# Graph attention on one core: probabilities turned by DMA transposes instead of TensorE, and heads stacked by VectorE

## What is computed

```python
h = jnp.maximum(_layernorm(x, axis=-1), 0.0)
q, k, v = (_heads(h @ W + b) for W, b in ((Wq, bq), (Wk, bk), (Wv, bv)))
scores = jnp.einsum('bhqd,bhkd->bhqk', q, k) / np.sqrt(HEAD_SIZE)
bias = jnp.where(graph_mask, 0.0, NEG)[:, None]
probs = jax.nn.softmax(scores + bias, axis=-1)
ctx = jnp.einsum('bhqk,bhkd->bhqd', probs, v)
out = x + (ctx.transpose(0, 2, 1, 3).reshape(b, s, H) @ Wf + bf)
```

## Time and profile before

| | |
|---|---|
| median of 3 runs | 702.35 us (701.69 to 703.3) |
| profiled execution, first to last instruction | 701.6 us |
| mean granted clock of TensorE | 0.985 |
| bytes moved by DMA | 61.36 MB, 87 GB/s over the span |

### The profile page before, as it was taken

How to read it: one execution, slowest core, us unless ns; L and a number is a source line. 1 busy time by engine, 2 the same in 40 slices (tenths; PEclk the granted TensorE clock), 3 DMA queues, 4 the chain that set the end, 5 groups by cost and what they waited for, 6 DMA issues and landing times.

```text
span 701.6 us, 21244 instructions
## 1 busy us (share of the span) xinstructions
PE 677.3 (97%) x7156; PEld 562.7 (80%) x7156; DVE 555.2 (79%) x1676; ACT 464.9 (66%) x972; POOL 270.1 (39%) x330
## 2 busy tenths in 40 slices
PE   7688999999999999999999999999999999999996
PEld 5466888888888888888888888888888888888874
DVE  5748887887887878788787878878787887888785
ACT  2545676767677676767767676776767677676763
POOL 1334444334444433444443344444334444333420
PEclk8899999999999999999999999999999999999998
DMA  5123333433332343333234333323433332343220
GB/s 187 43 52 89 101 72 89 105 85 90 90 98 71 90 105 84 90 92 96 71 91 105 84 87 94 90 74 94 105 81 89 95 88 75 95 105 78 65 71 35
DMA packets 72453, 61.36 MB, mean 87 GB/s; under 512 B 17649, under 2 KB 72434, under 8 KB 72434
## 3 DMA queue, kind: packets, MB, share of 16 engines
q1 hardware_dynamic: 72434, 61.12, 33.8%
HBM read 17.05 MB, written 12.58 MB: 42 GB/s over the span
## 4 chain that ended last, share of the span: by engine, by line
PE 90%; issue 3%; DVE 3%; DMA 1%; ACT 1%; POOL 1%; SPq 0%; POOLq 0%; DVEq 0%
PE ring L767 17%; PE ring L769 17%; PE ring L768 17%; PE probs_t L834 11%; PE scores L824 6%; PE scores L825 6%; PE ctx L850 3%; PE ctx L852 3%; PE ctx L851 3%; PE ring L779 3%; PE ring L860 3%; DMA w_raw<-in_L_gnn_Wv_dram 1%; ACT probs L404 0%; DMA x_in<-in_x_dram 0%; DVE w_lo L623 0%
## 5 line engine op out<-in xcount | busy, mean ns | idle before, releaser
L404 ACT ACTIVATE probs<-logits,least 128x256 f32<-128x256 f32 x384 | 175.1, 504 | 78.0 <-DVE least L536 77.0
L354 POOL TENSOR_TENSOR split<-qk,split 128x512 f16<-128x512 f32 x96 | 111.3, 1160 | 274.9 <-DVE split L559 274.9
L409 ACT ACTIVATE pt_hi<-probs_t 128x512 f16<-128x512 f32 x192 | 114.6, 597 | 108.1 <-PE probs_t L834 107.3
L536 DVE CUSTOM_DVE_ANT_0 logits<-scores,mask,logit_unscale 128x256 f32<-128x256 f32 x384 | 169.1, 478 | 4.5 <-PE scores L825 3.7
L767 PE MATMUL ring<-h_hi,w_hi 128*128 128x256 f16 x576 | 158.3, 275 | 2.0 <-DVE w_lo L623 1.5
L768 PE MATMUL ring<-h_lo,w_hi 128*128 128x256 f16 x576 | 158.1, 275 | 0.0
L769 PE MATMUL ring<-h_hi,w_lo 128*128 128x256 f16 x576 | 158.0, 274 | 0.0
L543 DVE SCALAR_TENSOR_TENSOR pt_lo<-probs_t,pt_hi 128x512 f16<-128x512 f32 x192 | 131.6, 686 | 0.7 <-ACT pt_hi L409 0.6
L834 PE MATMUL probs_t<-ident,probs 128*128 128x128 f32 x768 | 116.4, 274 | 5.4 <-ACT probs L404 5.3
L559 DVE CAST split<-qk 128x512 f16<-128x512 f32 x96 | 41.3, 430 | 98.3 <-ACT qk L422 98.3
L422 ACT ACTIVATE qk<-ring,qk_bias_s,qkv_ratio 128x256 f32<-128x256 f32 x192 | 96.7, 552 | 15.2 <-PE ring L769 15.2
(11 more groups left out here) (86 smaller groups left out, 1300.0 us busy)
## 6 DMA issues: line engine op xcount, KB each, us to landing
heads<-split SPq DMA_DIRECT2D x192, 96.0 KB, 2.2
x_in<-in_x_dram SPq DMA_DIRECT2D x32, 384.0 KB, 3.3
heads<-split SPq DMA_DIRECT2D x192, 64.0 KB, 2.1
out_dram<-result SPq DMA_DIRECT2D x64, 192.0 KB, 1.9
adj_in<-in_adj_dram SPq DMA_DIRECT2D x32, 64.0 KB, 2.0
w_raw<-in_L_gnn_Wq_dram SPq DMA_DIRECT2D x1, 576.0 KB, 4.1
w_raw<-in_L_gnn_Wk_dram SPq DMA_DIRECT2D x1, 576.0 KB, 6.5
w_raw<-in_L_gnn_Wv_dram SPq DMA_DIRECT2D x1, 576.0 KB, 6.3
```

The lines of the kernel that those rows point to most:

```text
L404: act.activation(probs[u % 2][:, a], logits[u % 2][:, a], ACT.Exp, bias=least[u % 2][:, a:a + 1], scale=-1.0).then_inc(probs_ready, 1)
L536: dve.tensor_tensor_reduce(out=logits[u % 2][:, a], in0=score_bank[u % 2][:, a * S:(a + 1) * S], in1=mask[b.parity][:, t], scale=logit_uns ...
```

## The change

Six parts, all in one:

1. The turn of the probabilities leaves PE. `exps` now computes p x 2^14 directly (its bias is `least` plus ln 2^14, made per unit by a small ACT instruction into `raised`). ACT `probs_hi` splits off the high part and POOL `probs_lo` the low part, both from SBUF and with queries still in the partitions, into `p_rows[u]` (128 x 1024 f16, 256 KB). SP then issues one DMA transpose per unit, which writes `p_cols[u]`. DVE's `probs_lo` is gone.
2. `apply_probs` comes four slots after the scores (`LAG = 4`) instead of two, and everything behind it moves accordingly: `divide`, `transpose_context`, `project_out` and `finish` of a batch are done in the next cycles, and there is one cycle more at the end (`B + 2`).
3. The heads of all three pairs are stacked by DVE, `copy_heads`, four copies of 64 partitions per pair (two of 768 columns and two of 512), in place of the twelve DMAs.
4. `x_in` and `residual` have four buffers (`RING`) instead of two, `h_hi` and `h_lo` two, `logits`, `least` and `probs` three, and the loop turns four batches at a time.
5. The two PSUM banks of the turned probabilities go to the ring of the projections (five banks).
6. The order within the cycles is rewritten on all five engines; `project_v(b, 1)` moves into batch b's own first slot, and `layer_stats` looks three batches ahead, in two parts.

The diff, cut to its core:

```diff
@@
+            def transpose_probs(b, u):
+
+                wait(sp, p_lo_ready, b.count(UNITS, u + 1))
+                alone(sp)
+                sp.dma_start_transpose(p_cols[u][:].rearrange("p w a s q -> p (w a s) q"),
+                                       p_rows[u][:].rearrange("p w a k -> p (w a k)")).then_inc(p_placed[u], 16)
@@
+            def probs_lo(b, u):
+                wait(pool, p_hi_ready, b.count(UNITS, u + 1))
+                pool.tensor_tensor(p_rows[u][:, 1], probs[u % 3][:], p_rows[u][:, 0],
+                                   ALU.subtract).then_inc(p_lo_ready, 1)
@@
             def exps(b, u):
 
+                wait(act, p_lo_ready, b.count(UNITS, u - 2))
+                wait(act, logits_ready, b.count(2 * UNITS, 2 * u + 2))
+                alone(act)
+                act.activation(raised[u % 3][:], least[u % 3][:], ACT.Identity,
+                               bias=p_raise[:, 0:1]).then_inc(raised_ready, 1)
+                wait(act, raised_ready, b.count(UNITS, u + 1))
@@
             def probs_hi(b, u):
-                wait(act, pt_ready, b.count(UNITS, u + 1))
-                act.activation(pt_hi[u % 2][:].rearrange("p a t q -> p (a t q)"), pt_bank[u % 2][:],
-                               ACT.Copy, scale=P_SCALE).then_inc(pt_hi_ready, 1)
+                wait(act, probs_ready, b.count(2 * UNITS, 2 * u + 2))
+                act.activation(p_rows[u][:, 0], probs[u % 3][:], ACT.Copy).then_inc(p_hi_ready, 1)
@@
                 if u == 0:
                     wait(dve, mask_ready, b.count(2, 2))
+                wait(dve, probs_ready, b.count(2 * UNITS, 2 * u - 4))
@@
-            def probs_lo(b, u):
-                wait(dve, pt_hi_ready, b.count(UNITS, u + 1))
-                dve.scalar_tensor_tensor(
...
+            def copy_heads(b, j):
+
+                wait(dve, qk_lo_ready, b.count(C, j + 1))
+                for a in range(2):
+                    own = slice(D * a, D * a + D)
+                    other = slice(D - D * a, 2 * D - D * a)
+                    dst, src = heads[b.parity][:, 2 * j + a], split[j]
+                    dve.tensor_copy(dst[own], src[own, 1:4]).then_inc(heads_copied, 1)
+                    dve.tensor_copy(dst[other, 0:2], src[own, 0:3:2]).then_inc(heads_copied, 1)
@@
             def scores(b, u):
                 t, j = u // C, u % C
                 if t == 0:
-                    wait(pe, heads_placed[j], b.count(4 * 16, 4 * 16))
+                    wait(pe, heads_copied, b.count(4 * C, 4 * (j + 1)))
                 wait(pe, logits_ready, b.count(2 * UNITS, 2 * u - 2))
@@
-            def transpose_probs(b, u):
-                wait(pe, pt_lo_ready, b.count(UNITS, u - 1))
...
             def apply_probs(b, u):
                 t, j = u // C, u % C
-                wait(pe, pt_lo_ready, b.count(UNITS, u + 1))
+                wait(pe, p_placed[u], b.count(16, 16))
@@
+                def attend(u):
+
+                    if here:
+                        scores(b, u)
+                    if u < LAG:
                         if before:
-                            transpose_probs(b + -1, UNITS - 1)
+                            apply_probs(b + -1, UNITS - LAG + u)
                     elif here:
-                        transpose_probs(b, u - 1)
+                        apply_probs(b, u - LAG)
```

More of the change, by code:

```diff
@@ L23 @@
+import math
 from contextlib import ExitStack
@@ L376, in cycle @@
             def cycle(b):
-                first, front = b.k == -1, (b + 1).exists()
+                here, before, front = b.exists(), (b + -1).exists(), (b + 1).exists()
+                first = b.k == -1
+                if here:
+                    split_lo(b, 2)
+                if before:
+                    probs_lo(b + -1, 5)
+                if here:
+                    probs_lo(b, 0)
+                if (b + 2).exists():
+                    normalise(b + 2)
+                if here:
+                    probs_lo(b, 1)
                 if front:
@@ L380, in cycle @@
                     split_lo(b + 1, 0)
+                if here:
+                    probs_lo(b, 2)
+                if front:
                     split_lo(b + 1, 1)
-                    if not first:
-                        add_bias(b + 1)
-                if (b + 2).exists():
-                    normalise(b + 2)
-                if front:
-                    split_lo(b + 1, 2)
                     if first:
@@ L391, in cycle @@
                         pool.wait_ge(bf_ready, 1)
-                        add_bias(b + 1)
+                if here:
+                    probs_lo(b, 3)
+                if front:
+                    add_bias(b + 1)
+                if here:
+                    probs_lo(b, 4)
             cycles(pool, cycle)
@@ L588, in finish, with layer_stats @@
                 dve.scalar_tensor_tensor(out=result[t][:], in0=R_OUT[t][:, 0:H], scalar=out_unscale[:, 0:1],
-                                         in1=residual[b.parity][:, t], op0=ALU.mult,
+                                         in1=residual[b.slot][:, t], op0=ALU.mult,
                                          op1=ALU.add).then_inc(result_ready, 1)
-            def layer_stats(b):
-                wait(dve, x_loaded[b.parity], b.dma_count())
-                for t in range(QT):
-                    dve.bn_stats(out=stats[:, t], in_=x_in[b.parity][:, t]).then_inc(moments, 1)
+            def layer_stats(b, parts):
+                if 0 in parts:
+                    wait(dve, x_loaded[b.slot], b.dma_count(RING))
+                for t in parts:
+                    dve.bn_stats(out=stats[:, t], in_=x_in[b.slot][:, t]).then_inc(moments, 1)
+                if 1 not in parts:
+                    return
                 for t in range(QT):
@@ L784, in project_qk @@
                     wait(pe, h_lo_ready, b.count(2, 2))
-                if j == 2 and 0 in parts:
-                    wait(pe, qk32_ready, b.count(2 * C, 4))
+                if 0 in parts and j > 0 and (b + -1).exists():
+                    wait(pe, v_lo_ready, (b + -1).count(2, j))
                 for n in parts:
@@ L865, in project_out @@
                 wait(pe, ct_lo_ready, b.count(2, t + 1))
-                if t == 1 and (b + 2).exists():
-                    wait(pe, qk32_ready, (b + 2).count(2 * C, 2))
                 for c in range(C):
@@ L909, in cycle @@
-                if here:
-                    scores(b, 0)
-                transpose_of(0)
-                apply_of(0)
+                        apply_probs(b, u - LAG)
+                attend(0)
                 if front and not first:
                     transpose_h(b + 1)
+                if here:
+                    project_v(b, 1)
+                attend(1)
+                if front:
+                    project_qk(b + 1, 0)
+                attend(2)
+                if before:
+                    transpose_context(b + -1, 0)
```

362 lines of the change are left out of this document (158 added, 204 removed).

## The result

The changed kernel is **slower by 13%**. Its four runs took 810.72, 810.55, 798.5 and 794.03 us, against a median of 702.83 us for the kernel before on the same chip. The ratio is 1.1323 (interval 1.1281 to 1.1365), taken from the two shorter runs, so about 796 against 703, while the profiled execution is one of the two longer ones (810.55 us, span 808.8, clock 0.92 against 0.94). The forecast was 743 with a range of 640 to 850.

A forecast was written before the change was run, and what follows sets the result against it. PE set the 20.60 us period before; DVE was to bound the changed kernel at 16.3 work + 5.4 waits = 21.7 us. 32 x 21.7 + 42.4 start and drain + 5 ends + 0.75 to the median = 743 us, range 640 to 850.

The forecast's parts named there:

- PE, removed: Turns of probs leave PE: 2.64 us a batch saved, PE's need falls from 20.60 to 17.96 us, 617 us at best.
- The forecast's base: Period before the change, from 20 batches in 412.0 us: 20.60 us a batch, set by PE alone.
- ACT and POOL: Added splits and `raised`: ACT rises from 14.36 to 17.4 us a batch, POOL from 8.36 to 15.3, both under 17.96.
- The copies: Twelve head copies a batch on DVE: 3.9 us, less 0.07 overlap each, so 3.1; DVE's work 16.3 us.
- the low end: DVE copies move four f16 columns at a time: 0.36 and 0.29 us, against 0.96 and 0.69 at the high end.
- DVE against POOL: DVE's copies and casts wait for POOL's wide operations at the shared port: 5.4 us a batch, range 0 to 19.7.
- The step that failed: DVE's work plus waits, 16.3 + 5.4 = 21.7 us a batch, taken as the period, making DVE the bound.
- SP and the DMA engines: Six transposes a batch replace twelve heads DMAs: 1.0 to 8.4 us each, taken as hidden by the lag of some 7 us.
- Rival 1: Copies find the port free; faster if waits stay below 4.1 us a batch, 647 us at 2.4; chance 0.33.
- Rival 2: DMA transposes bound the kernel if each takes over 3.6 us; 855 us at 4.2 us each; chance 0.10.
- rival 3: Gain and loss cancel at waits of about 4.1 us a batch, nothing measurable (about 0.2%); chance 0.03.
- What would show it: Signs: PE some 83% busy, idle before `scores` from DVE, copies 0.7 us or more, casts over 0.43, POOL about 490 us.

The follow-up runs named there:

- e16: Changed kernel with heads of pairs 0 and 1 by DMA ahead of the transposes, pair 2 by VectorE, loop written out; 685.01 us, ratio 0.9756 to the kernel before.
- e4: Kernel before, with only the heads stacked by VectorE copies instead of DMAs, the copies ahead of the rest in their slots; 806.14 us, ratio 1.1459.
- e1: Changed kernel with GpSimd's low part of the probabilities left out but for two columns; 734.12 us, ratio 1.0413 to the kernel before.
- e5: Changed kernel with `ct_lo` put first in slot 4 on VectorE, ahead of result and copies; 765.27 us, ratio 1.0893 to the kernel before.
- e6: Changed kernel with the low part of the probabilities on VectorE instead of GpSimd; 834.16 us, ratio 1.1875 to the kernel before.
- e9: Changed kernel with `ct_lo` first in slot 4 and the copies of pair 0 ahead of the cast; 782.39 us, ratio 1.1121 to the kernel before.
- e13: Changed kernel with `ct_lo` first in slot 4 and GpSimd's residual behind the low part there; 762.32 us, ratio 1.0841 to the kernel before.
- e15: Kernel before, with only the heads stacked by VectorE copies, the copies behind the rest in their slots; 888.37 us, ratio 1.2636.
- e14: Changed kernel with eight matmuls nobody reads on TensorE ahead of the second output projection; 772.29, 772.49 and 778.1 us, ratio 1.1016 to the kernel before.
- e8: Changed kernel with all heads by DMA again and GpSimd's low part cut to two columns; 725.08 us, ratio 1.0323 to the kernel before.
- e2: Changed kernel with the heads stacked by twelve DMAs a batch again, GpSimd's low part kept; 726.86 us, ratio 1.0337 to the kernel before.
- e10: Changed kernel with heads of pairs 0 and 1 by DMA ahead of the transposes, pair 2 by VectorE; 701.45 us, ratio 0.998 to the kernel before.
- e18: Kernel before with the loop written out; 703.04 us, ratio 0.9992 to the kernel before.

## Why the prediction was right in its direction and wrong in its size

**PE, removed.** Right as a term, never seen as time: 768 matmuls are gone, and in e16 TensorE is busy for 374.71 of 400 us, 18.3 of its period of 19.5 us, against the forecast 17.96. The forecast's base is 0.1 us off: the 412 us of the earlier trace rows hold 20.1 batches, since `rstd` starts at 200.99 and at 405.99 us, ten batches apart, so the period before was 20.50 us and not 20.60. The 3 us that this takes from 32 periods go to start and drain, so the sum stands.

**ACT and POOL.** Right: `raised` takes 296 ns (forecast 0.29), ACT's split 626 (forecast 710), GpSimd's low part 1170 (forecast 1160); GpSimd's busy time is 507 us (forecast about 490).

**The copies.** Right in the time of one: 0.34 to 0.36 and 0.29 us (forecast 0.36 and 0.29), so the low end holds; (0.36 - 0.29) / 256 is 0.27 ns a column, a quarter of the 1.07 of one column at a time. Wrong in the overlap: the forecast took 0.07 us off each copy, but four copies in a row take 1.40 us from the start of the first to the start of what follows them (418.43 to 419.83), 4.2 us for twelve, and are busy for 3.9 us a batch in e4 (forecast 3.1).

**DVE against POOL.** The mechanism is right, and shown from both sides: the copies' mean is 603 and 573 ns beside a busy GpSimd and 353 and 292 in e4, and their ends fall on GpSimd's. The rule of "SBUF — State Buffer", section "SBUF: two separate sides" in the Trainium skill, an exclusive lock for a whole instruction, fits these rows, but for the two-column `rstd`, which blocks nothing (a copy at 406.19 us took 0.36 beside one that ran from 405.98 to 406.72). That a queued GpSimd operation gets in between two queued copies is the rows' own. The size: (603 - 353) x 192 + (573 - 292) x 192 + (698 - 430) x 96 ns are 128 us, **4.0 us a batch instead of 5.4** (698 is the mean of the casts L596). The two errors partly cancel: 13.2 + 3.9 + 4.0 = 21.1 us, and the trace has VectorE busy for 20.9, against 21.7.

**The step that failed** is the sentence after that sum: "DVE's period is then 16.3 + 5.4 = 21.7 us". It took an engine's busy time as the period because that was true of TensorE before, where it ran without a gap. It is not true of VectorE, which hands something to TensorE, ACT and GpSimd and takes something from them in every slot. In the stretch of 200 to 600 us VectorE was busy for 349 of 400 us in the changed kernel, 360 in e1, 344 in e4, 368 in e5, 366 in e6, 367 in e9, 372 in e13 and 344 in e15: in none of the kernels that have all twelve copies on VectorE did it come over 93%. With the measured work the forecast's own arithmetic gives 32 x 20.9 + 42.4 + 5 + 0.75 = 717 us; the 79 us from there to 796 are idle time, a term that the forecast put at nothing. Two effects on it are measured, one at a time and not as a sum: 31 us for the place of the copies ahead of `ct_lo` (e5), 18 to 24 us for filling TensorE's wait (e14), which is put down to the clock that TensorE loses behind its waits; the two overlap, since e5 raised the clock too. e4 shows that the lock is not needed for such idle time, and e15 that the opposite order of the copies does not avoid it.

Why idle time comes at all is read from the waits, not tested by itself. A sum over a batch lets an engine catch up in one slot what it lost in another. In e4 and in the changed kernel TensorE waits in the slots where copies stand ahead of `ct_lo` or the result, and VectorE waits in others, each for the other or for ScalarE. The time is then nearer to a sum of the slower engine slot by slot than to the larger of two sums over the batch.

**SP and the DMA engines.** Hidden, as forecast: a transpose lands in 3.1 us, TensorE hardly waits for one, and queue 1's share is 47.0%. By that the estimate of 10.5 us from "VectorE: DVE Perf Modes", section "The three transpose paths" in the Trainium skill, falls, and the rule of the Trainium skill's page "Advanced Engine Details and Errata", section "X-Bar Transpose (TRN2)", as fast as an ordinary DMA, holds roughly for the landing: the 256 KB lie between a store of 192 KB that lands in 1.8 us and `x_in` with 384 KB, which lands in 3.3. What I had not priced is SyncE's own time for issuing one, 1.25 us. No wait of the changed kernel shows it, but in e8, and probably in e2, SyncE's issues are the bound.

**The rivals.** Rival 1 wanted waits below 4.1 us a batch. They were 4.0, on its threshold, and the time was far on the other side, because both the rival and the forecast shared the failed step. Rival 2 (the transposes) and rival 3 (a tie) did not occur. **What would show it** had PE at 83% (81), idle time in front of `scores` behind DVE (50.2 us, but 77.1 in front of the projection was larger and was not named), and copies of 0.7 us or more (0.60 and 0.57).

## What to carry to other kernels

The busy time of an engine is a period only if the trace shows that engine without gaps. When a change moves the bound from a feeder that runs free (TensorE) to an engine in the middle of every chain (VectorE), expect idle time on top of its work (VectorE was idle for 7 to 14% of the time here), and look for what stands in its line ahead of the operation that TensorE wants next. Work that waits for nothing and is wanted late belongs on a queue with room: two thirds of the copies moved to DMAs were worth 95 us here, and all of them moved only 70, probably since SyncE's issues then became the bound. Count slot by slot, not over a batch: a forecast that compares sums over a batch misses what one slot cannot give to the next (read from the waits here, not tested).

## What the runs showed of the hardware

- A DMA transpose of 128 x 1024 f16 lands in 3.1 us and holds SyncE's queue for 1.25 us; an ordinary DMA held it for 0.4 to 0.63 us.
- An f16 copy on VectorE of 64 partitions takes 0.34 us for 768 columns and 0.29 us for 512 when nothing meets it, and up to 1.31 us beside GpSimd.
- Back-to-back VectorE copies and back-to-back GpSimd operations alternated, one of each, in the stretch of 413 to 417 us, so that four copies in a row took up to 0.34 + 1.14 + 1.20 + 0.98 us.
- Useless matmuls in a wait of TensorE made the kernel 18 to 24 us faster, with the granted clock at 0.97 to 0.98 instead of 0.94.
- The branch of a loop added some 3.9 us to the batch that it fell in in e10, some 1.8 in the changed kernel, and nothing in the kernel before, whose time did not change without it (e18).
